# An fp32 conditioning layer with LoRA experts and a low-rank FFN: part of the transposes moved from TensorE to VectorE and the transfer queue

## The chip, the cores and the metric

The kernel runs on one core of a Trainium2 chip. The time is the device time of one execution in microseconds. The kernel before takes 154.18 us, the median of three runs (153.75 to 154.49). The profiled execution took 154.44 us.

The engines are named as in the profile: PE is TensorE, DVE is VectorE, ACT is ScalarE, POOL is GpSimd and SP is SyncE, which here only issues transfers.

## What is computed

There are 2048 tokens (32 x 64) of width 1024, in fp32. In short form:

```python
base   = x @ W.T                                   # (2048, 1024)
logits = x @ Wr.T + 5 * one_hot(language_id, 8)
gates  = softmax over the top 2 logits, 0 elsewhere
h      = einsum('btd,erd->bter', x, A)             # 8 experts, rank 16
cond   = base + 2 * einsum('bter,bte,eor->bto', h, gates, B)
out    = x + cond @ (U * S @ V.T).T                # rank 256
```

Only 256 numbers per token pass through the low rank. So the kernel forms the projection W.T V once (1024 x 256), and per token z = x (W.T V) + 2 (gates * h) (B V), and out = x + z (U S).T. B V, here bv, is 128 x 256.

## The kernel before, in words

**Precision.** PE multiplies in fp32r. Each fp32 operand is split into a rounded part (ACT, a copy, suffix hi) and the rest (DVE or POOL, a subtraction, suffix lo). Each product is three matmuls, `triple` (lines 342 to 345).

**Tiles.** 16 tiles of 128 tokens, worked on in 8 pairs (PAIRS). x^T of a tile comes from HBM into a ring of four (XTR), is split by ACT (split_x, line 609) and POOL (split_x, line 279). The plain x comes into x_all, a ring of six, and takes the result in place.

**Per tile**, `project(t)` (line 408) multiplies x^T as stationary operand by 264 columns: 128 for h, 8 for the logits, 128 for the first half of z. The result has tokens in the partitions, in bank pj[t % 2]. DVE turns the logits into gates in 11 small steps (gates_top, gates_apply, lines 772 to 804; one exponential on ACT, exp_top, line 661) and writes the gated h into gh.

**Per pair**, `half_t(p)` (line 425) forms the second half of z with the columns of z in the partitions, for both tiles at once. The last products need z this way round. The first half is in the other layout, so ACT copies it out of pj (copy_z, line 657) and PE transposes it into zt (line 434). In the same way gh is transposed (transpose_gh, line 442) into bank gt, split, and multiplied with bv onto zt (`mix`, line 450). mix(p) runs in the middle of project(2p + 2).

**The output product** uses Strassen's scheme in Winograd's form: 7 products of 128 x 128 x 512 (p1 to p7) where 8 would be plain. DVE forms four sums of z blocks (sums, line 827) and ACT and DVE split them (split_zb). `first_part(p)` is p1, p6, p7, p5, p2 and `second_part(p)` is p4, p3. p2 needs copy_u: ACT copies p1 out of bank_a before p2 is added there. DVE adds p6 and p7 to it (`up`, line 841), then adds the banks to x (xb1, xa0, xb0, xa1), and POOL adds the two upper sums (sides, line 306). The product lags two pairs behind the projections. The last pair is multiplied in the plain way (expand).

**Order.** Each engine has its own list, written out by hand, and waits on semaphores. PE's loop over pairs is lines 553 to 562: project(2p), first_part(p - 2), project(2p + 1), second_part(p - 2), zt_free(p), half_t(p), transpose_gh(p). ACT's is pair (line 665), DVE's pair_2 (line 876) and pair (line 893), POOL's lines 330 to 337. SP issues the loads and stores in the order of lines 242 to 250.

Of the kernel before, what the change touches and what calls it, by code (L numbers as in the profile page):

```python
# [16 lines left out]
def adaln_ffn(nc, xt, x, ids, VW, W, AW, B, U, S, out):  # L17
# [28 lines left out]
    with ExitStack() as ctx:  # L46
# [115 lines left out]
        x22_copied = sem("x22_copied")  # L162
# [178 lines left out]
        def _(pe):  # L341
# [66 lines left out]
            def project(t):  # L408
                q, r = t % 2, t % XTR
                pe.wait_ge(xt_lo, t + 1)  # L410
                if t >= 2:
                    pe.wait_ge(gh_done, t - 1)
                    pe.wait_ge(z_copied, t - 1)
                for k in range(DC):
# [6 lines left out]
                    if t >= 2 and t % 2 == 0 and k == MH:  # L421
                        mix(t // 2 - 1)
                last.then_inc(pj_done, 1)

            def half_t(p):
                r = (2 * p) % XTR
                dst = zt_v[:, 1, :, :]
                for k in range(DC):
                    last = triple(dst, proj_hi[:, k, TCOLS:COLS], proj_lo[:, k, TCOLS:COLS],
                                  xT_hi[:, r:r + 2, k, :], xT_lo[:, r:r + 2, k, :], k == 0, False, shared=True)  # L430
                    if k == MH + 1:
                        pe.wait_ge(z_copied, 2 * p + 2)
# [570 lines left out]
```

## Time and profile before

| | |
|---|---|
| median of three runs | 154.18 us |
| profiled execution | 154.44 us |
| its span, first to last instruction | 152.7 us |
| PE busy | 147.4 us, 97% |
| PE weight loads busy | 139.1 us, 91% |
| DVE busy | 107.2 us, 70% |
| POOL busy | 72.3 us, 47% |
| ACT busy | 63.5 us, 42% |
| moved by DMA | 32.72 MB, 214 GB/s on average |

A row of the time line gives the start in us from the span's start, how long it lasted, the engine, the line of the kernel, the operation, what it writes and reads with the shapes, and how many such instructions are merged in it. In brackets stands the idle time ahead and what ended it. The durations of matmuls overlap, so the step from start to start is what one costs. "q" behind an engine is its queue: there the duration is that of issuing a transfer. The table by stretch gives the stretch, its length, and per engine the busy us and the number of instructions (PE, PE's weight loads, DVE, ACT, POOL), then the clock granted to PE as a share of full speed, the DMA engines' busy share and GB/s.

### The profile page before, as it was taken

Reading aid. Unit: us, or ns where it says so; the run is one execution under the profiler, and the core shown is the slowest. Engines: PE = TensorE matmul, PEld = TensorE weight load, DVE = VectorE, ACT = ScalarE, POOL = GpSimd, SP = SyncE. Lnnn points to the kernel's source line nnn. Section 1 sums busy time; section 2 is a strip of 40 time slices with the busy share of each in tenths; the row PEclk is TensorE's granted clock in tenths of the full one; section 3 lists DMA queues with packets and bytes.
Section 4 is the critical chain, followed back from the end, with each engine's and each line's share of the span. In section 5 each row is a group of like instructions: output and inputs, shape, how many; then the busy total and the mean of one; then the engine's idle time right before and its main releaser. Section 6 shows DMA issues by size and latency. Waiting matters only on the chain.

```text
span 152.7 us, 2912 instructions
## 1 busy us (share of the span) xinstructions
PE 147.4 (97%) x1056; PEld 139.1 (91%) x1056; DVE 107.2 (70%) x297; ACT 63.5 (42%) x141; POOL 72.3 (47%) x57
## 2 busy tenths in 40 slices
PE   7799999999999999999999999999999999999991
PEld 5699999999999989998999899989999998998880
DVE  0488887759478999978765875587558736795851
ACT  4397876894546422446014612351334105013000
POOL 2000242993560659292966186636655640721700
PEclk9999999999999999999999999999999999999998
DMA  5999999999303030049719903980591068006184
GB/s 171 315 400 409 400 405 411 410 407 409 132 6 137 0 137 4 0 192 345 288 60 350 386 34 136 338 347 10 211 286 57 0 277 262 17 0 275 69 339 142
DMA packets 10670, 32.72 MB, mean 214 GB/s; under 512 B 1441, under 2 KB 1953, under 8 KB 10529
## 3 DMA queue, kind: packets, MB, share of 16 engines
q1 hardware_dynamic: 10368, 31.96, 55.8%
q10 hardware_dynamic: 288, 0.59, 1.2%
q8 instruction: 8, 0.13, 0.3%
q14 instruction: 6, 0.04, 0.1%
HBM read 24.16 MB, written 8.39 MB: 213 GB/s over the span
## 4 chain that ended last, share of the span: by engine, by line
PE 93%; DMA 3%; ACT 0%; DVE 0%; SPq 0%; issue 0%; DVEq 0%
PE fin L343 13%; PE fin L345 13%; PE fin L344 13%; PE pj L344 10%; PE pj L343 10%; PE pj L345 10%; PE zt L343 6%; PE zt L345 6%; PE zt L344 6%; DMA w_raw<-in_W 3%; PE gt L447 1%; PE zt L434 1%; PE fin L380 1%; PE gt L344 1%; PE gt L345 1%; PE fin L390 1%
## 5 line engine op out<-in xcount | busy, mean ns | idle before, releaser
L281 POOL TENSOR_TENSOR xT_lo<-xt_raw,xT_hi 128x1024 fp32r<-128x1024 f32 x15 | 36.5, 2443 | 25.2 <-DVE gh L801 7.9
L304 POOL TENSOR_TENSOR x_all<-x_all,vw_raw 128x512 f32<-128x512 f32 x21 | 26.6, 1297 | 25.8 <-DVE vw_raw L849 25.8
L343 PE MATMUL pj<-proj_hi,xT_hi 128*128 128x264 f32 x128 | 36.9, 288 | 0.0
L344 PE MATMUL pj<-proj_lo,xT_hi 128*128 128x264 f32 x128 | 36.3, 284 | 0.0
L345 PE MATMUL pj<-proj_hi,xT_lo 128*128 128x264 f32 x128 | 36.2, 283 | 0.0
L343 PE MATMUL fin<-v_hi,w_hi 128*128 128x256 f32 (+1 forms) x80 | 25.7, 321 | 0.0
L344 PE MATMUL fin<-v_lo,w_hi 128*128 128x256 f32 (+1 forms) x80 | 25.6, 320 | 0.0
L345 PE MATMUL fin<-v_hi,w_lo 128*128 128x256 f32 (+1 forms) x80 | 25.6, 320 | 0.0
L344 PEld LDWEIGHTS pj<-proj_lo,xT_hi 128*128 128x128 f32 x128 | 24.1, 189 | 0.2
L343 PEld LDWEIGHTS pj<-proj_hi,xT_hi 128*128 128x128 f32 x128 | 24.1, 188 | 0.2
L345 PEld LDWEIGHTS pj<-proj_hi,xT_lo 128*128 128x128 f32 x128 | 24.0, 188 | 0.0
L343 PE MATMUL zt<-xT_hi,proj_hi 128*128 128x256 f32 x64 | 18.6, 291 | 0.0
L855 DVE TENSOR_TENSOR x_all<-fin,x_all 128x512 f32<-128x512 f32 x28 | 17.9, 682 | 0.0
L344 PE MATMUL zt<-xT_lo,proj_hi 128*128 128x256 f32 x64 | 17.9, 280 | 0.0
L345 PE MATMUL zt<-xT_hi,proj_lo 128*128 128x256 f32 x64 | 17.9, 280 | 0.0
L613 ACT CAST xT_hi<-xt_raw 128x1024 fp32r<-128x1024 f32 x16 | 16.8, 1048 | 0.6 <-DMA xt_raw<-in_xt 0.5
L345 PEld LDWEIGHTS fin<-v_hi,w_lo 128*128 128x128 f32 x80 | 15.2, 191 | 1.2
L343 PEld LDWEIGHTS fin<-v_hi,w_hi 128*128 128x128 f32 x80 | 15.2, 190 | 0.9
L344 PEld LDWEIGHTS fin<-v_lo,w_hi 128*128 128x128 f32 x80 | 15.2, 190 | 0.8
L659 ACT COPY z_sb<-pj 128x128 f32<-128x128 f32 x16 | 4.3, 266 | 22.4 <-DVE logit L776 22.4
L344 PEld LDWEIGHTS zt<-xT_lo,proj_hi 128*128 128x128 f32 x64 | 12.0, 188 | 0.3
L343 PEld LDWEIGHTS zt<-xT_hi,proj_hi 128*128 128x128 f32 x64 | 12.0, 188 | 0.2
(100 smaller groups left out, 282.5 us busy)
## 6 DMA issues: line engine op xcount, KB each, us to landing
xt_raw<-in_xt SPq DMA_DIRECT2D x16, 512.0 KB, 7.6
x_all<-in_x SPq DMA_DIRECT2D x16, 512.0 KB, 6.5
out<-x_all SPq DMA_DIRECT2D x13, 512.0 KB, 3.2
vw_raw<-in_VW SPq DMA_DIRECT2D x6, 384.0 KB, 7.1
w_raw<-in_W SPq DMA_DIRECT2D x8, 256.0 KB, 6.6
out<-x_all SPq DMA_DIRECT2D x5, 256.0 KB, 2.0
w_raw<-in_U SPq DMA_DIRECT2D x1, 1024.0 KB, 8.8
aw_raw<-in_AW SPq DMA_DIRECT2D x1, 544.0 KB, 7.2
```

The lines of the kernel that those rows point to most:

```text
L281: nc.gpsimd.tensor_sub(xT_lo[:, t % XTR, :, :], xt_raw[:, t % XTR, :, :], xT_hi[:, t % XTR, :, :].bitcast(F32)).then_inc(xt_lo, 1)
L304: nc.gpsimd.tensor_add(x_all[:, t % XR, cols], x_all[:, t % XR, cols], ups[:, j, :]).then_inc(side_add, 1)
L343: nc.tensor.matmul(dst, l_hi, r_hi, start=first, stop=False, skip_group_check=shared)
L344: nc.tensor.matmul(dst, l_hi, r_lo, start=False, stop=False, skip_group_check=shared)
L345: return nc.tensor.matmul(dst, l_lo, r_hi, start=False, stop=last, skip_group_check=shared)
L380: nc.tensor.matmul(p_dst(h, m), w_hi[:, i % WRING, cols], v_hi[:, k, :], start=False, stop=False, skip_group_check=True)
L390: last = nc.tensor.matmul(p_dst(h, m), w_lo[:, i % WRING, cols], v_hi[:, k, :], start=False, stop=True, skip_group_check=True)
L434: nc.tensor.matmul(zt_v[:, 0, t, :], z_sb[:, t, :], ident[:, :], start=False, stop=False, is_transpose=True, skip_group_check=True)
L447: last = nc.tensor.transpose(gt[:, t * P:(t + 1) * P], gh[:, t, :], ident[:, :])
L613: nc.scalar.copy(xT_hi[:, t % XTR, :, :], xt_raw[:, t % XTR, :, :]).then_inc(xt_hi, 1)
L659: nc.scalar.copy(z_sb[:, t % 2, :], pj[t % 2][:, Z0:TCOLS]).then_inc(z_copied, 1)
L855: nc.vector.tensor_add(x_all[:, t % XR, cols], src[:, :], x_all[:, t % XR, cols]).then_inc(fin_read, 1)
```

## The change

- In pairs 1 to 6 neither z nor gh is transposed by PE. DVE transposes their 32 x 32 blocks in place of the whole (turn_z from PSUM, turn_gh from SBUF) into blk. SP moves the 12 blocks off the diagonal to their place in tr with 12 transfers of 32 x 4 x 128 bytes a pair, ACT copies the 4 on the diagonal.
- gh is split from tr (split_gh_moved), and mix(p - 1) runs in pair p behind first_part(p - 2). The first half of z is added to zt in PSUM by DVE (add_z0) behind it. z has two banks (zt and gt) now, so that two pairs can be under way.
- The z split of a pair follows a pair later, in two steps: the first takes three blocks (split_z_parts), the second four. The four sums read their operands from PSUM.
- half_t(p) runs directly behind the two projections. x^T is loaded and split a pair sooner (POOL's waits between the splits go).
- Pair 0 and pair 7 keep PE's transposes.

The core of the diff; SQ is 32, SQS 4 and MOVES 192:

```diff
+        zs = w_flat[:, 0:8 * P].rearrange("p (j n) -> p j n", n=P)
+        blk = w_flat[:, 8 * P:16 * P].rearrange("p (q m n) -> p q m n", q=2, m=4)
+        tr = w_flat[:, 16 * P:24 * P].rearrange("p (q m n) -> p q m n", q=2, m=4)
...
         bv_ps = gt[:, RANK:2 * RANK]
-        zt_v = zt[:, :].rearrange("p (m t n) -> p m t n", m=MC, t=2)
+        zt_bank = [zt, gt]
+        zt_v = [b[:, :].rearrange("p (m t n) -> p m t n", m=MC, t=2) for b in zt_bank]
...
+            def move_blocks(p):
+                sp.wait_ge(blk_done, 3 * p)
+                for i in range(SQS):
+                    for j in range(SQS):
+                        if i != j:
+                            sp.dma_start(tr[SQ * j:SQ * (j + 1), p % 2, :, SQ * i:SQ * (i + 1)],
+                                         blk[SQ * i:SQ * (i + 1), p % 2, :, SQ * j:SQ * (j + 1)]).then_inc(tr_load[p % 2], 16)
+
             for p in range(1, PAIRS):
-                if 2 * p + XTR < TILES:
-                    load_xt(2 * p + XTR)
-                    load_xt(2 * p + 1 + XTR)
+                if p == 1:
+                    load_xt(2 + XTR)
+                    load_xt(3 + XTR)
+                if 2 * p + 2 + XTR < TILES:
+                    load_xt(2 * p + 2 + XTR)
+                    load_xt(2 * p + 3 + XTR)
+                if p < PAIRS - 1:
+                    move_blocks(p)
                 if 2 * p >= XR:
                     load_x(2 * p)
                     load_x(2 * p + 1)
...
-            pool.wait_ge(tl_done, 2)
             split_x(5)
             pool.wait_ge(us_lo_done, MC)
+            split_x(6)
+            split_x(7)
             for p in range(2, PAIRS):
-                if p < PAIRS - 1:
-                    split_x(2 * p + 2)
+                if p < PAIRS - 2:
+                    split_x(2 * p + 4)
                 sides(p - 2)
-                if p < PAIRS - 1:
-                    pool.wait_ge(gh_done, 2 * p + 2)
-                    split_x(2 * p + 3)
+                if p < PAIRS - 2:
+                    split_x(2 * p + 5)
...
                     pe.wait_ge(gh_done, t - 1)
+                if 2 <= t < 4:
                     pe.wait_ge(z_copied, t - 1)
...
-                    if t >= 2 and t % 2 == 0 and k == MH:
-                        mix(t // 2 - 1)
+                    if t == 2 and k == MH:
+                        mix(0)
...
-                    if k == MH + 1:
-                        pe.wait_ge(z_copied, 2 * p + 2)
+                    if k == MH - 1 and p == PAIRS - 1:
+                        mix(p - 1)
+                    if k == MH + 1 and (p == 0 or p == PAIRS - 1):
+                        pe.wait_ge(z_copied, 2 if p == 0 else 4)
...
             def zt_free(p):
-                pe.wait_ge(za_lo, p)
-                pe.wait_ge(sums_done, 4 * p)
+                if p == 1:
+                    pe.wait_ge(bv_lo_done, 1)
+                if p >= 2:
+                    pe.wait_ge(za_lo, p - 1)
+                    pe.wait_ge(sums_done, 4 * (p - 1))
...
                 project(2 * p)
+                project(2 * p + 1)
+                zt_free(p)
+                half_t(p)
                 if p >= 2:
                     first_part(p - 2)
-                project(2 * p + 1)
+                if 3 <= p < PAIRS - 1:
+                    mix(p - 1)
+                if p == PAIRS - 1:
+                    transpose_gh(p)
                 if p >= 2:
                     second_part(p - 2)
-                zt_free(p)
-                half_t(p)
-                transpose_gh(p)
+                if p == 2:
+                    mix(1)
...
+            def split_z_parts(p):
+                act.wait_ge(z0_done, p)
+                zh_free(p)
+                nc.scalar.copy(zh[:, p % 2, 0:MC, :], zt_v[p % 2][:, :, 0, :])
+                nc.scalar.copy(zh[:, p % 2, MC, :], zt_v[p % 2][:, 1, 1, :])
+                nc.scalar.copy(zs[:, MC, :], zt_v[p % 2][:, 1, 1, :]).then_inc(za_hi, 1)
...
+            def split_gh_moved(p):
+                act.wait_ge(tr_load[p % 2], MOVES * ((p + 1) // 2))
+                act.wait_ge(tr_diag, SQS * p)
+                nc.scalar.copy(ghT_hi[:, :], tr[:, p % 2, 0:2, :]).then_inc(gt_hi, 1)
+
+            def move_diagonal(p):
+                act.wait_ge(blk_done, 3 * p)
+                for i in range(SQS):
+                    rows = slice(SQ * i, SQ * (i + 1))
+                    nc.scalar.copy(tr[rows, p % 2, :, rows], blk[rows, p % 2, :, rows]).then_inc(tr_diag, 1)
 
...
             def pair(p):
-                if p < PAIRS - 1:
-                    split_x(2 * p + 2)
-                split_za(p - 1)
-                copy_x22(p - 1)
+                exp_top(2 * p)
+                exp_top(2 * p + 1)
+                if p >= 3:
+                    split_gh_moved(p - 1)
+                if p < PAIRS - 2:
+                    split_x(2 * p + 4)
                 copy_u(p - 2)
+                if p == 2:
+                    split_gh_moved(1)
+                move_diagonal(p)
+                split_z_parts(p - 1)
+                if p < PAIRS - 2:
+                    split_x(2 * p + 5)
+                split_zb(p - 1)
+
+            def last_pair(p):
                 copy_z(2 * p)
                 exp_top(2 * p)
-                split_zb(p - 1)
-                if p < PAIRS - 1:
-                    split_x(2 * p + 3)
+                split_gh_moved(p - 1)
                 copy_z(2 * p + 1)
                 exp_top(2 * p + 1)
+                split_z_parts(p - 1)
+                copy_u(p - 2)
+                split_zb(p - 1)
                 split_gh(p)
...
             split_t(1)
-            copy_z(2)
+            split_x(5)
             exp_top(2)
             split_zb(0)
-            copy_z(3)
             exp_top(3)
-            split_x(5)
-            split_gh(1)
-            for p in range(2, PAIRS):
+            move_diagonal(1)
+            split_x(6)
+            split_x(7)
+            for p in range(2, PAIRS - 1):
                 pair(p)
+            last_pair(PAIRS - 1)
...
+            def turn_z(t):
+                nc.vector.transpose(blk[:, (t // 2) % 2, 2 + t % 2, :], pj[t % 2][:, Z0:TCOLS]).then_inc(blk_done, 1)
+
+            def turn_gh(p):
+                dve.wait_ge(gh_done, 2 * p + 2)
+                nc.vector.transpose(blk[:, p % 2, 0:2, :], gh[:, :, :]).then_inc(blk_done, 1)
...
+            def split_gh_moved(p):
+                dve.wait_ge(gt_hi, p + 1)
+                nc.vector.tensor_sub(ghT_lo[:, :].rearrange("p (t n) -> p t n", t=2), tr[:, p % 2, 0:2, :],
+                                     ghT_hi[:, :].bitcast(F32).rearrange("p (t n) -> p t n", t=2)).then_inc(gt_lo, 1)
...
+            def sums_first():
+                nc.vector.tensor_add(zs[:, 3, :], zt_v[0][:, 0, 1, :], zs[:, 2, :]).then_inc(sums_done, 1)
+                dve.wait_ge(sums_done, 1)
+                nc.vector.tensor_sub(zs[:, 4, :], zs[:, 3, :], zt_v[0][:, 0, 0, :]).then_inc(sums_done, 1)
+                dve.wait_ge(sums_done, 2)
+                nc.vector.tensor_sub(zs[:, 5, :], zs[:, 2, :], zs[:, 4, :]).then_inc(sums_done, 1)
+                nc.vector.tensor_sub(zs[:, 6, :], zt_v[0][:, 1, 0, :], zs[:, 4, :]).then_inc(sums_done, 1)
...
+            def add_z0(p):
+                dve.wait_ge(zt_done, p + 1)
+                dve.wait_ge(tr_load[p % 2], MOVES * ((p + 1) // 2))
+                dve.wait_ge(tr_diag, SQS * p)
+                nc.vector.tensor_add(zt_v[p % 2][:, 0, :, :], zt_v[p % 2][:, 0, :, :], tr[:, p % 2, 2:4, :]).then_inc(z0_done, 1)
 
             def sums(p):
                 n = 4 * p
-                nc.vector.tensor_add(zs[:, 1, :], zt_v[:, 0, 1, :], zs[:, 0, :]).then_inc(sums_done, 1)
+                z = zt_v[p % 2]
+                dve.wait_ge(za_hi, p + 1)
+                nc.vector.tensor_add(zs[:, 3, :], z[:, 0, 1, :], zs[:, MC, :]).then_inc(sums_done, 1)
...
-                nc.vector.tensor_sub(zs[:, 3, :], zs[:, 0, :], zs[:, 2, :]).then_inc(sums_done, 1)
-                nc.vector.tensor_sub(zs[:, 4, :], zt_v[:, 1, 0, :], zs[:, 2, :]).then_inc(sums_done, 1)
+                nc.vector.tensor_sub(zs[:, 5, :], z[:, 1, 1, :], zs[:, 4, :]).then_inc(sums_done, 1)
+                nc.vector.tensor_sub(zs[:, 6, :], z[:, 1, 0, :], zs[:, 4, :]).then_inc(sums_done, 1)
+
+            def split_z_parts(p):
+                nc.vector.tensor_sub(zl[:, p % 2, 0:MC, :], zt_v[p % 2][:, :, 0, :],
+                                     zh[:, p % 2, 0:MC, :].bitcast(F32))
+                nc.vector.tensor_sub(zl[:, p % 2, MC, :], zt_v[p % 2][:, 1, 1, :],
+                                     zh[:, p % 2, MC, :].bitcast(F32)).then_inc(za_lo, 1)
...
+            def gates(t):
+                gates_top(t)
+                if 2 <= t < TILES - 2:
+                    turn_z(t)
+                gates_apply(t)
+
             def pair_2():
                 split_zb(0)
                 split_us(1)
-                split_za(1)
+                gates(4)
+                gates(5)
+                turn_gh(2)
                 up(0, 1)
                 up(0, 2)
                 xb1(0)
-                sums(1)
-                gates_top(4)
-                gates_apply(4)
-                gates_top(5)
-                gates_apply(5)
+                split_gh_moved(1)
                 xa0(0)
                 xb0(0)
+                add_z0(1)
                 xa1(0)
-                split_gh(2)
+                sums(1)
+                split_z_parts(1)
 
             def pair(p):
+                gates(2 * p)
                 split_zb(p - 2)
-                split_za(p - 1)
-                sums(p - 1)
-                gates_top(2 * p)
-                gates_apply(2 * p)
+                gates(2 * p + 1)
+                turn_gh(p)
+                split_gh_moved(p - 1)
                 up(p - 2, 1)
                 up(p - 2, 2)
                 xb1(p - 2)
                 xa0(p - 2)
-                gates_top(2 * p + 1)
-                gates_apply(2 * p + 1)
+                add_z0(p - 1)
+                xb0(p - 2)
+                sums(p - 1)
+                split_z_parts(p - 1)
+                xa1(p - 2)
+
+            def last_pair(p):
+                gates(2 * p)
+                split_zb(p - 2)
+                split_gh_moved(p - 1)
+                gates(2 * p + 1)
+                add_z0(p - 1)
+                sums(p - 1)
+                up(p - 2, 1)
+                up(p - 2, 2)
+                xb1(p - 2)
+                xa0(p - 2)
+                split_z_parts(p - 1)
+                split_zb(p - 1)
+                split_gh(p)
                 xb0(p - 2)
                 xa1(p - 2)
-                if p == PAIRS - 1:
-                    split_zb(p - 1)
-                split_gh(p)
...
-            sums(0)
-            gates_top(2)
-            gates_apply(2)
-            gates_top(3)
-            gates_apply(3)
+            sums_first()
+            gates(2)
+            gates(3)
+            turn_gh(1)
             split_t(1)
-            split_gh(1)
             pair_2()
-            for p in range(3, PAIRS):
+            for p in range(3, PAIRS - 1):
                 pair(p)
+            last_pair(PAIRS - 1)
```

## Rows read from the trace of the kernel before

**Rows 1.** Section 1 of the page: busy time, share of the span, instructions.
```profile
PE 147.4 (97%) x1056; PEld 139.1 (91%) x1056; DVE 107.2 (70%) x297; ACT 63.5 (42%) x141; POOL 72.3 (47%) x57
```

**Rows 2.** Table by stretch, pair 2's stretch and a later pair's.
```profile
50.00:64.50 14.50, 14.50 (x105) 13.65 (x104) 13.36 (x33) 5.23 (x13) 8.79 (x6) 1.00 0.10 37
79.10:93.68 14.58, 14.58 (x105) 13.73 (x105) 9.71 (x33) 5.04 (x13) 8.64 (x6) 1.00 0.59 216
```

**Rows 3.** Time line of PE, the transposes of z and gh of pair 1.
```profile
49.29 0.28 PE L345 MATMUL zt<-xT_hi,proj_lo 128*128 128x256 f32 x1
49.40 0.38 PE L434 MATMUL zt<-ident,z_sb 128*128 128x128 f32 x2
...
49.74 0.28 PE L344 MATMUL zt<-xT_lo,proj_hi 128*128 128x256 f32 x1
...
50.34 0.38 PE L447 MATMUL gt<-ident,gh 128*128 128x128 f32 x2
```

**Rows 4.** Time line of PE, first and last product of two runs of 15.
```profile
43.28 0.28 PE L343 MATMUL pj<-proj_hi,xT_hi 128*128 128x264 f32 x1
...
44.97 0.28 PE L345 MATMUL pj<-proj_hi,xT_lo 128*128 128x264 f32 x1
...
54.17 0.40 PE L343 MATMUL fin<-us_hi,w_hi 128*128 128x512 f32 x1
...
57.35 0.39 PE L345 MATMUL fin<-us_hi,w_lo 128*128 128x512 f32 x1
```

**Rows 5.** Time line of DVE between 46 and 61 us.
```profile
46.08 0.15 DVE L776 SCALAR_TENSOR_TENSOR logit<-target,pj 128x8 f32<-128x8 f32 x1
...
46.59 0.23 DVE L781 TENSOR_SCALAR dtop<-top 128x2 f32<-128x2 f32 x1
...
46.99 0.17 DVE L784 TENSOR_TENSOR chosen<-iota_e,top_i 128x16 f32<-128x16 f32 x1
...
47.92 0.15 DVE L776 SCALAR_TENSOR_TENSOR logit<-target,pj 128x8 f32<-128x8 f32 x1
...
54.06 1.21 DVE L759 TENSOR_TENSOR us_lo<-vw_raw,us_hi 128x1024 fp32r<-128x1024 f32 x1
...
55.81 1.49 DVE L849 TENSOR_TENSOR vw_raw<-fin,vw_raw 128x512 f32<-128x512 f32 x2 [0.20 <-PE fin L345]
...
57.81 0.28 DVE L829 TENSOR_TENSOR zs<-zt,zs 128x128 f32<-128x128 f32 x1
...
59.78 0.55 DVE L781 TENSOR_SCALAR dtop<-top 128x2 f32<-128x2 f32 x1
...
60.50 1.10 DVE L784 TENSOR_TENSOR chosen<-iota_e,top_i 128x16 f32<-128x16 f32 x1
```

**Rows 6.** Time line of POOL between 43 and 62 us.
```profile
43.40 2.41 POOL L281 TENSOR_TENSOR xT_lo<-xt_raw,xT_hi 128x1024 fp32r<-128x1024 f32 x1 [1.16 <-DVE v_lo L812]
51.06 2.40 POOL L281 TENSOR_TENSOR xT_lo<-xt_raw,xT_hi 128x1024 fp32r<-128x1024 f32 x1 [5.25 <-DVE v_lo L812]
55.35 2.41 POOL L281 TENSOR_TENSOR xT_lo<-xt_raw,xT_hi 128x1024 fp32r<-128x1024 f32 x1 [1.90 <-DVE us_lo L759]
57.71 3.85 POOL L304 TENSOR_TENSOR x_all<-x_all,vw_raw 128x512 f32<-128x512 f32 x3
```

**Rows 7.** Time line of ACT between 43 and 56 us.
```profile
43.90 1.06 ACT L623 CAST v_hi<-vw_raw 128x1024 fp32r<-128x1024 f32 x1
...
48.69 0.20 ACT L663 ACTIVATE etop<-dtop 128x2 f32<-128x2 f32 x1 [0.32 <-DVE dtop L781]
48.89 1.04 ACT L613 CAST xT_hi<-xt_raw 128x1024 fp32r<-128x1024 f32 x1
...
55.06 0.59 ACT L651 COPY vw_raw<-fin 128x512 f32<-128x512 f32 x1 [0.62 <-PE fin L345]
```

**Rows 8.** Time line of SP's queue, the x^T loads of one pair.
```profile
66.93 2.02 SPq L202 DMA_DIRECT2D xt_raw<-in_xt  x2
```

**Rows 9.** Table by stretch, behind PE's last product, which ends at 149.3.
```profile
151.00:151.50 0.50, 0.00 (x0) 0.00 (x0) 0.00 (x0) 0.00 (x0) 0.00 (x0) 0.71 0.28 88
```

More of the change, by code:

```diff
@@ L157, in adaln_ffn @@
         gt_done = sem("gt_done")
+        blk_done = sem("blk_done")
+        tr_load = [sem("tr_load0"), sem("tr_load1")]
+        tr_diag = sem("tr_diag")
         gt_hi = sem("gt_hi")
@@ L161, in adaln_ffn @@
         zt_done = sem("zt_done")
-        x22_copied = sem("x22_copied")
+        zb_copied = sem("zb_copied")
+        z0_done = sem("z0_done")
         sums_done = sem("sums_done")
@@ L181, in adaln_ffn @@
         LAG = 4
+        SQ = 32
+        SQS = P // SQ
+        MOVES = 16 * SQS * (SQS - 1)
         PRODS = 7
@@ L426, in half_t @@
                 r = (2 * p) % XTR
-                dst = zt_v[:, 1, :, :]
+                dst = zt_v[p % 2][:, 1, :, :]
                 for k in range(DC):
@@ L438, in zt_free @@
             def zt_free(p):
-                pe.wait_ge(za_lo, p)
-                pe.wait_ge(sums_done, 4 * p)
+                if p == 1:
[3 more added lines that the diff above has]
+                    pe.wait_ge(sums_done, 4 * (p - 1))
             def transpose_gh(p):
+                dst = gt if p == 0 else pj[0]
                 pe.wait_ge(gh_done, 2 * p + 2)
-                if p >= 1:
-                    pe.wait_ge(gt_lo, p)
                 for t in range(2):
-                    last = nc.tensor.transpose(gt[:, t * P:(t + 1) * P], gh[:, t, :], ident[:, :])
+                    last = nc.tensor.transpose(dst[:, t * P:(t + 1) * P], gh[:, t, :], ident[:, :])
                 last.then_inc(gt_done, 1)
@@ L455, in mix @@
                     cols = slice(m * P, (m + 1) * P)
-                    last = triple(zt[:, 2 * m * P:2 * (m + 1) * P], bv_hi[:, cols], bv_lo[:, cols],
+                    last = triple(zt_bank[p % 2][:, 2 * m * P:2 * (m + 1) * P], bv_hi[:, cols], bv_lo[:, cols],
                                   ghT_hi[:, :], ghT_lo[:, :], False, True, shared=True)
@@ L631, in split_za @@
                 zh_free(p)
[L632 removed]
+                nc.scalar.copy(zh[:, p % 2, 0:MC, :], zt_v[p % 2][:, :, 0, :]).then_inc(za_hi, 1)
+            def split_z_parts(p):
[4 more added lines that the diff above has]
+                nc.scalar.copy(zs[:, MC, :], zt_v[p % 2][:, 1, 1, :]).then_inc(za_hi, 1)
             def split_zb_plain(p):
                 act.wait_ge(za_lo, p + 1)
[L636 to L641 removed]
+                nc.scalar.copy(zh[:, p % 2, MC:2 * MC, :], zt_v[p % 2][:, :, 1, :]).then_inc(zb_hi, 1)
             def split_zb(p):
                 act.wait_ge(sums_done, 4 * p + 4)
[L645 removed]
+                if p == 0:
+                    nc.scalar.copy(zh[:, 0, 2:7, :], zs[:, 2:7, :]).then_inc(zb_hi, 1)
+                else:
+                    nc.scalar.copy(zh[:, p % 2, 3:7, :], zs[:, 3:7, :]).then_inc(zb_hi, 1)
+            def split_gh_moved(p):
[7 more added lines that the diff above has]
+                    nc.scalar.copy(tr[rows, p % 2, :, rows], blk[rows, p % 2, :, rows]).then_inc(tr_diag, 1)
             def copy_u(p):
@@ L653, in split_gh @@
             def split_gh(p):
-                act.wait_ge(gt_done, p + 1)
-                nc.scalar.copy(ghT_hi[:, :], gt_both).then_inc(gt_hi, 1)
+                act.wait_ge(gt_done, 1 if p == 0 else 2)
+                nc.scalar.copy(ghT_hi[:, :], (gt if p == 0 else pj[0])[:, 0:2 * P]).then_inc(gt_hi, 1)
             def copy_z(t):
@@ L721, in _ @@
             split_za(0)
-            copy_x22(0)
+            nc.scalar.copy(zs[:, 2, :], zt_v[0][:, 1, 1, :]).then_inc(zb_copied, 1)
             split_t(1)
-            copy_z(2)
+            split_x(5)
             exp_top(2)
             split_zb(0)
-            copy_z(3)
             exp_top(3)
-            split_x(5)
-            split_gh(1)
-            for p in range(2, PAIRS):
+            move_diagonal(1)
+            split_x(6)
+            split_x(7)
+            for p in range(2, PAIRS - 1):
                 pair(p)
+            last_pair(PAIRS - 1)
             copy_u(PAIRS - 2)
@@ L837, in split_zb @@
                 dve.wait_ge(zb_hi, p + 1)
-                nc.vector.tensor_sub(zl[:, p % 2, 2:7, :], zs[:, :, :],
-                                     zh[:, p % 2, 2:7, :].bitcast(F32)).then_inc(zb_lo, 1)
+                first = 2 if p == 0 else 3
+                nc.vector.tensor_sub(zl[:, p % 2, first:7, :], zs[:, first:7, :],
+                                     zh[:, p % 2, first:7, :].bitcast(F32)).then_inc(zb_lo, 1)
             def up(p, j):
```

24 lines of the change are left out of this document (8 added, 16 removed).

## The prediction

> **What bounds the kernel now.** I read the page's busy times first: TensorE (PE) is busy for 147.4 of 152.7 us [rows 1]. The table by stretch then shows that this is no average over gaps: in a later pair (79.1 to 93.7) PE is busy 14.58 of 14.58 us, and in the stretch from 50 to 64.5 us 14.50 of 14.50, while VectorE (DVE) has 13.36 us of work there against 9.71 in that later pair [rows 2]. The reader is to see two things. Only PE work that disappears can shorten a pair; and the stretch in which pairs 1 and 2 meet is the one where a second engine is nearly full.
>
> The steps of PE come from start to start of instructions. One 264-wide product takes 0.121 us (14 steps from 43.28 to 44.97) and one 512-wide product 0.227 (14 steps from 54.17 to 57.35) [rows 4]. The 256-wide ones I put at 0.118. A pair is 48 x 0.121 + 30 x 0.118 + 21 x 0.227 = 14.1 us, and the rest of its 14.58, some 0.46, is four PE transposes.
>
> **What the change removes.** The two z transposes stand between starts 49.29 and 49.74: 0.45 us less two plain steps of 0.12 is 0.21; the pair sum above gives 0.23 [rows 3, 4]. The two gh transposes (first at 50.34) have the same shape. Both go in pairs 1 to 6: 12 x (0.21 to 0.24) = 2.5 to 2.9 us, taken as **2.7**. All of it is on the path, since PE has no gap there. Pairs 0 and 7 keep theirs. The two copies of z on ScalarE (ACT) that go cost nothing now: ACT waits.
>
> **What it adds on DVE, and the steady pairs 3 to 5.** Times here count from the first product of the pair. PE: two projections to 5.8, half_t to 8.6, five products to 12.0, the LoRA product (mix) to 12.7, two products to 14.1. New on DVE are turn_z (twice), turn_gh, add_z0, and one more part of the split. A DVE transpose has no row. The nearest are the 128x128 add from PSUM, 0.28 us, for turn_z, and between that and the 128x1024 subtraction, 1.21, for turn_gh [rows 5]; I take 0.3 and 0.4, of which 0.2 and 0.35 count from start to start. Bounds: 0.15 (a 128x8 operation) to 0.6 for each turn_z. Together with add_z0 that is about 1.5 us more in a pair of which DVE fills 9.7 of 14.6 us [rows 2]. It is hidden, if the order fits:
> Gates take 1.84 us (46.08 to 47.92) [rows 5], 2.05 with the turn. Gates of tile 2p start at 3.1. GpSimd (POOL) still splits the x of the pair before until about 4.6, which delays this gates' dtop (why, below). They end at about 5.9, the z split at 6.65, the second gates at 8.7, turn_gh at 9.1, the split of the moved gh at 9.5. POOL's next x split starts when half_t has freed x^T and ACT has split it, at 8.8 + 1.05 + 0.1 = 9.9 [rows 7]. So the gh split is through with 0.4 us to spare. ACT copies u at 9.9 to 10.4, the two sums from PSUM take 1.5 [rows 5] and are done at 12.0, before p4 at 12.7. add_z0, sums and z split follow and end at about 2.8 in the next pair. Nothing stalls PE; cost **0**. If the spare 0.4 us is gone, see rival 3.
>
> **Pair 2, the step that decides.** The new order puts POOL's splits of tiles 5, 6 and 7 earlier and back to back, and lets them fall on DVE's gates. The rows show what that does. With POOL idle dtop takes 0.23 us (46.59) and chosen 0.17 (46.99). While POOL runs three additions in a row (57.71, 3.85 for three, so they end at 58.99, 60.28, 61.56), dtop at 59.78 takes 0.55 and ends at 60.33, just behind the second; chosen at 60.50 takes 1.10 and ends at 61.60, just behind the third [rows 5, 6]. A DVE operation of these kinds waits for the end of the running POOL operation, and the next POOL operation gets in ahead of the one after. An x split holds POOL for 2.41 us [rows 6], so it can cost the gates twice that.
>
> The list, from the rows:
> - ACT's split_x(5) follows its split at 43.90 and is done at 45.9; POOL splits tile 5 at 46.0 to 48.4. Before, that split stood at 51.06, behind DVE's last v_lo [rows 6, 7]. Gates of tile 2 start at 46.08; dtop now ends at 48.4 and the gates at 49.85 instead of 47.92.
> - DVE then has gates(3) to 51.9, turn_gh to 52.3, split_t(1) 1.2, z split 0.8 (640 elements, between the rows), split_us(1) 1.2: end at 55.4. Before it was 54.06 + 1.21 = 55.27 [rows 5].
> - At 55.4 the last wait of POOL is met, and it splits tiles 6 and 7: 55.5 to 57.9, 57.95 to 60.35. (Before, one split stood at 55.35 and DVE had PSUM work beside it.) DVE comes with gates(4): dtop, due at 55.9, ends at 57.95; chosen waits to 60.35; the gates end at 61.5 instead of 57.4. gates(5): 61.5 to 63.55.
> - On ACT copy_u(0) now stands behind exp_top(5) and split_x(8). ACT is free 0.97 us after the gates begin (48.89 against 47.92) [rows 5, 7]: 62.5; split_x(8) to 63.5, copy_u(0) to 64.1.
> - PE: gh transposes at 50.34 [rows 3] less the 0.22 saved put project(4) at 50.1; two projections and half_t end at 58.7; p1, p6, p7, p5 end at 61.4. p2 needs copy_u(0) and starts at 64.15: **2.7 us** idle. The sums from PSUM end at 64.9 and 65.6; p4 was due at 64.8: **0.8** more. p3 is just met. mix(1) needs DVE's gh split, which comes at 66.2, when POOL (x split to 66.05) has started its first side addition, 1.28 us: gh ready at 67.85, **0.85** idle, or nothing if DVE gets in first.
> Together 3.5 to 4.35 us, taken as **3.9**. PE is full in the pairs after, so nothing is given back. Without any POOL block copy_u(0) would be ready at 60.5 and the stall would be zero: the price hangs on the block alone.
>
> **SP's queue.** Each pair gets 12 transfers of 16 KB, between the x^T loads and the x loads, behind a wait for turn_gh (9.1). x^T loads now run a pair ahead; their waits (POOL's splits of two tiles back) are met before. The stores of x behind the moves need xa1 at 16.8 anyway. An issue behind others takes 1.0 us (2.02 for two) [rows 8]; the lower bound is a third of that, since the moves carry little. At 0.45 the moves are issued by 14.5 and needed at 21.8 (ACT's gh split of the next pair), so cost 0. At 1.0 they are issued at 21.1, which is rival 4.
> The Trainium skill (DMA: Bandwidth & Descriptors, section Bandwidth) says that transfers under 64 KB are dominated by their descriptors, and its fit for one DMA (section Anatomy of one DMA) is about 2.0 us plus bytes over 436 GB/s. One after the other that makes 12 x 2.04 = 24.5 us a pair as an estimate, more than the pair has. The fit is for one transfer at a time, and no row here shows 16 KB transfers in a train; it is why rival 4 has a chance at all.
>
> **The end.** Pair 7 keeps its PE work. p1(6) needs a z split that ends at 14.4 of the pair, and is due at 14.55: 0. The next z split (two SBUF operands) is due at 14.35, and POOL's third side addition at 14.4, so p6(6) may wait up to 1.2 us: **0.6** taken, 0 and 1.2 kept.
>
> **Sum** against the profiled execution: span 152.7 - 2.7 + 3.9 + 0.6 = 154.5; around the span lie 154.44 - 152.7 = 1.74 us, so 156.24. The median shown, 154.18, is 0.26 under the profiled execution: **156.0**, 1.2% slower.
>
> **Rivals.**
> 1. No lock in pair 2 (the gates get in between, or POOL starts behind them), the transposes' gain stays: 152.7 - 2.7 + 1.74 - 0.26 = **151.5**. For it: VectorE's instructions are short, and half a microsecond in the order decides. Against: rows 59.78 and 60.50 show both waits, and POOL's start 0.08 after split_us (55.35 against 55.27) comes ahead of dtop, due 0.5 after. Chance 0.22.
> 2. Only the first of the two waits bites: gates(4) end at 59.25, copy_u(0) at 62.0; p2 0.6 late, p4 0.7. With 0.6 to 1.2 at the other places the gain is cancelled: **153.4 to 154.9**, no change. Chance 0.13.
> 3. The forecast and more: DVE's gh split in pairs 3 to 5 comes behind POOL's x split at 9.9 (turns of 0.45 us do it) and waits to 12.3; p4 then starts at 13.8 instead of 12.7, 1.1 us in each of three pairs, so **159.3**. Or PE's clock: it is at full speed to 151 us and at 0.71 in the half microsecond behind [rows 9], that is, it begins to fall to 1.2 from 2.4 GHz under two microseconds after PE's last product. An idle gap of 2.7 us could do the same; three microseconds at half speed would cost 1.5: **157.5**. Both are slower; 0.2 in all.
> 4. The moves are late. SP would need 12 x 1.0 + 5 = 17 us for a pair of 14.1; 3 us in five pairs: over **168**. Against it: the trains of full 512 KB loads are the slowest thing in the queue. Chance 0.05.
> The forecast itself, within 154.9 to 157: 0.4.
>
> **Numbers.** A measurement of this kernel can tell about 0.5% (0.77 us) from no change. Faster is rival 1 and the lucky edge of 2: 0.23. Same: 0.13. Slower: 0.64. The likeliest case alone ranges over 154.9 to 157.0; for 8 in 10 I need rival 1 at one end and the two of rival 3 nearly at the other: 151.3 to 158.6.
>
> **What would show it.** In the trace after: no transposes in pairs 1 to 6 and steady pairs of 14.1 us; dtop and chosen of tile 4 with 2 us each; the copy of u of pair 0 behind the exp of tile 5; a PE gap of 2 to 3 us in front of the second half of bank_a's sum near 61 to 64 us. Wrong would be: chosen of tile 4 with 0.17 us, PE without a gap there, a pair of 14.5 or more from 70 us on, or an ACT wait on tr_load.

## The result and the profile after

The changed kernel takes 155.01 us, the median of 20 runs (153.78 to 155.98); the kernel before takes 153.99 in 20 runs beside them (153.24 to 154.66). The ratio is 1.0069, 95% interval 1.0047 to 1.0092: slower, by more than chance, and by about half of the 1.2% forecast. Here and below a median is of all runs, and a ratio, with its 95% interval, leaves out runs more than 1.5% above the fastest of their kernel.

The profiled execution took 154.07 us with a span of 152.3, which is 0.4 us *less* than the span of before. That is no contradiction. The 20 runs fall into two groups by the mean clock that PE was granted: ten at 0.998 or more (153.78 to 155.83, median 154.27) and ten at 0.986 to 0.988 (155.01 to 155.98, median 155.67). The profile shows one of the first group.

Busy times on the page, and two stretches of 14 us (stretch, length, then PE, PE's weight loads, DVE, ACT, POOL, the granted clock, DMA share, GB/s). They answer to [rows 1] and [rows 2]. The second stretch lies in later pairs, where nothing stalls.

```profile
PE 145.6 (96%) x1032; PEld 136.0 (89%) x1032; DVE 118.4 (78%) x327; ACT 68.2 (45%) x159; POOL 72.1 (47%) x57
```

```profile
50.00:64.00 14.00, 11.64 (x82) 10.37 (x81) 13.16 (x34) 6.58 (x17) 6.84 (x3) 1.00 0.32 93
106.00:120.00 14.00, 14.00 (x100) 13.16 (x99) 11.02 (x39) 5.08 (x16) 7.58 (x5) 1.00 0.53 165
```

A late pair is as full of PE work as before, with 24 matmuls fewer in the whole kernel. From one p1 to the next it now takes 14.17 us (89.50 to 117.85 for two pairs), where before it took 14.58 (83.33 to 127.08 for three). The loss is all in the first stretch: PE works for 11.64 of 14 us. Its three gaps, in the time line of PE (the bracket gives the idle time and who ended it), are these:

```profile
62.46 0.47 PE L365 MATMUL fin<-us_hi,w_hi 128*128 128x512 f32 x1 [1.87 <-ACT vw_raw L699]
...
63.89 0.51 PE L365 MATMUL fin<-v_hi,w_hi 128*128 128x512 f32 x1 [0.49 <-DVE vw_raw L946]
...
65.87 0.39 PE L365 MATMUL gt<-ghT_hi,bv_hi 128*128 128x256 f32 x1 [0.32 <-DVE ghT_lo L881]
```

These are p2, p4 and mix(1). Measured from start to start, less the plain step, they cost 2.03, 0.66 and 0.48 us, 3.2 together. What is behind them stands in the lines of DVE, POOL and ACT, against [rows 5], [rows 6] and [rows 7]:

```profile
54.04 0.15 DVE L837 SCALAR_TENSOR_TENSOR logit<-target,pj 128x8 f32<-128x8 f32 x1
...
54.55 2.07 DVE L842 TENSOR_SCALAR dtop<-top 128x2 f32<-128x2 f32 x1
...
56.80 2.18 DVE L845 TENSOR_TENSOR chosen<-iota_e,top_i 128x16 f32<-128x16 f32 x1
...
59.83 0.15 DVE L837 SCALAR_TENSOR_TENSOR logit<-target,pj 128x8 f32<-128x8 f32 x1
...
62.34 1.49 DVE L946 TENSOR_TENSOR vw_raw<-fin,vw_raw 128x512 f32<-128x512 f32 x2
```

```profile
54.20 4.75 POOL L303 TENSOR_TENSOR xT_lo<-xt_raw,xT_hi 128x1024 fp32r<-128x1024 f32 x2 [6.78 <-DVE us_lo L820]
```

```profile
60.60 0.20 ACT L711 ACTIVATE etop<-dtop 128x2 f32<-128x2 f32 x1 [3.64 <-DVE dtop L842]
...
60.80 1.03 ACT L645 CAST xT_hi<-xt_raw 128x1024 fp32r<-128x1024 f32 x1
61.74 0.57 ACT L699 COPY vw_raw<-fin 128x512 f32<-128x512 f32 x1
```

The reader is to see that an operation on 128 x 2 numbers lasts 2.07 us and one on 128 x 16 lasts 2.18, that the first ends at 56.62 and the second at 58.98, and that POOL's two splits end at about 56.6 and 58.95. The gates of tile 4 take 5.8 us (54.04 to 59.83); those of tile 5, which meet no split, take 2.0. On ACT the exp, the x split and the copy of u follow one after the other behind the dtop of tile 5.

### The profile page after: what moved, and what is told of

It reads as the page before. It is cut to its first block, busy times and chain, and to the rows that moved or that the text cites. A ratio compares the mean times of both kernels' runs of the same rounds, so it can differ in the third digit from the quotient of the medians.

```text
span 152.3 us, 2976 instructions
## 1 busy us (share of the span) xinstructions
PE 145.6 (96%) x1032; PEld 136.0 (89%) x1032; DVE 118.4 (78%) x327; ACT 68.2 (45%) x159; POOL 72.1 (47%) x57
## 4 chain that ended last, share of the span: by engine, by line
PE 83%; DVE 12%; issue 1%; ACT 1%; DVEq 1%; POOL 0%; POOLq 0%
PE fin L365 12%; PE fin L367 12%; PE fin L366 12%; PE pj L366 8%; PE pj L365 8%; PE pj L367 8%; PE gt L365 3%; PE gt L367 3%; PE gt L366 3%; DVE dtop L842 3%; PE zt L367 3%; PE zt L365 2%; PE zt L366 2%; PE fin L567 2%; DVE chosen L845 2%
## 5 line engine op out<-in xcount | busy, mean ns | idle before, releaser
L303 POOL TENSOR_TENSOR xT_lo<-xt_raw,xT_hi 128x1024 fp32r<-128x1024 f32 x15 | 35.9, 2407 | 33.8 <-ACT xT_hi L645 20.3
L365 PE MATMUL pj<-proj_hi,xT_hi 128*128 128x264 f32 x128 | 36.4, 284 | 0.0
L326 POOL TENSOR_TENSOR x_all<-x_all,vw_raw 128x512 f32<-128x512 f32 x21 | 27.3, 1328 | 19.0 <-DVE vw_raw L946 19.0
L952 DVE TENSOR_TENSOR x_all<-fin,x_all 128x512 f32<-128x512 f32 x28 | 18.5, 683 | 1.2 <-POOL x_all L326 0.8
L711 ACT ACTIVATE etop<-dtop 128x2 f32<-128x2 f32 x16 | 3.3, 203 | 29.4 <-DVE dtop L842 29.4
L946 DVE TENSOR_TENSOR vw_raw<-fin,vw_raw 128x512 f32<-128x512 f32 x14 | 9.7, 690 | 6.6 <-ACT vw_raw L699 5.8
L365 PE MATMUL fin<-us_hi,w_hi 128*128 128x512 f32 (+1 forms) x31 | 11.9, 382 | 1.9 <-ACT vw_raw L699 1.9
L842 DVE TENSOR_SCALAR dtop<-top 128x2 f32<-128x2 f32 x16 | 10.6, 664 | 1.5
L367 PE MATMUL fin<-us_hi,w_lo 128*128 128x512 f32 (+1 forms) x31 | 11.7, 378 | 0.0
L366 PE MATMUL fin<-us_lo,w_hi 128*128 128x512 f32 (+1 forms) x31 | 11.7, 376 | 0.0
```

The costliest lines, as they stand in the source:

```text
L303: nc.gpsimd.tensor_sub(xT_lo[:, t % XTR, :, :], xt_raw[:, t % XTR, :, :], xT_hi[:, t % XTR, :, :].bitcast(F32)).then_inc(xt_lo, 1)
L326: nc.gpsimd.tensor_add(x_all[:, t % XR, cols], x_all[:, t % XR, cols], ups[:, j, :]).then_inc(side_add, 1)
L365: nc.tensor.matmul(dst, l_hi, r_hi, start=first, stop=False, skip_group_check=shared)
L366: nc.tensor.matmul(dst, l_hi, r_lo, start=False, stop=False, skip_group_check=shared)
L367: return nc.tensor.matmul(dst, l_lo, r_hi, start=False, stop=last, skip_group_check=shared)
L711: nc.scalar.activation(etop[:, :], dtop[:, :], ACT.Exp, accum_out=esum[:, :]).then_inc(exp_done, 1)
```

## The experiments

e1, e2, e3 and e5 are the changed kernel with one thing different, e4 is e1 and e7 is e6 with one thing more, and e6 changes several things at once. The kernel before ran beside them on the same chip: 153.57 us beside e1 to e4 (33 runs), 153.66 beside e5 to e7 (11 runs, on another chip). The changed kernel itself did not run beside them, so it is compared with them by the ratios to before and by the traces, and not by the medians.

**e1: POOL behind the gates.**

```diff
             pool.wait_ge(us_lo_done, MC)
+            pool.wait_ge(gh_done, 6)
             split_x(6)
             split_x(7)
```

> The changed kernel, but GpSimd splits the x of tiles 6 and 7 only after the gates of tile 5 (one wait more). Theory A (the shared port: GpSimd's two splits hold the gates of tile 4, and everything behind them waits): dtop and chosen of tile 4 fall from 2.07 and 2.18 us to about 0.23 and 0.17, the gap of 2.0 us in front of p2 of pair 0 goes; a smaller one of up to 1 us may come at mix(1), where DVE's gh split meets the split of tile 7. Span about 2 to 3 us under the changed kernel's 152.3, median 152 to 153. Theory B (the list of ACT: copy_u(0) stands behind the exp of tile 5 and the x split, whatever the gates do): the gap stays above 1.5 us. Theory C (DVE has simply too much work in this pair): the gap stays, since no DVE work goes.

Measured: 153.00 us, ratio to before 0.9967 (0.9943 to 0.9991), span 151.0. The gates of tile 4 in its DVE line:

```profile
54.41 0.23 DVE L843 TENSOR_SCALAR dtop<-top 128x2 f32<-128x2 f32 x1
...
54.82 0.17 DVE L846 TENSOR_TENSOR chosen<-iota_e,top_i 128x16 f32<-128x16 f32 x1
...
61.42 1.63 DVE L882 TENSOR_TENSOR ghT_lo<-w_raw,ghT_hi 128x256 fp32r<-128x256 f32 x1
```

0.23 and 0.17, and the gap before p2 is gone. No DVE work was taken away and ACT's list was left as it was, so B (ACT's list) and C (too much work) fall as causes. But of the 3.2 us only half came off: POOL now splits tiles 6, 7 and 8 in one go (57.99, 7.32 us) and the block moves to the gh split, 1.63 us for 0.4 of work. PE loses 0.65 at mix(1), 0.43 at half_t(3) and 0.51 at p2 of pair 1, 1.6 together. So the span is 1.3 us under the changed kernel's, where theory A had said 2 to 3.

**e2: ACT copies u at once.**

```diff
                 exp_top(2 * p)
+                if p == 2:
+                    copy_u(0)
                 exp_top(2 * p + 1)
...
-                copy_u(p - 2)
+                if p >= 3:
+                    copy_u(p - 2)
```

> The changed kernel, but in pair 2 ACT copies p1 out of the bank before the exp of tile 5 and the x split. Theory A: p2 is no longer late, but the two sums from PSUM stand behind the gates of tile 5 on DVE and are still ready only at about 62.3 and 63.8, so p4 starts at the same time as now (63.9) and the time stays within 0.3 us of the changed kernel. Theory B: the gap of 2.0 us goes and the kernel is 2 us faster.

Measured: 153.52 us, ratio 0.9999 (0.9973 to 1.0025). Four of its 12 runs have a lowered clock; e7 comes back to them. In the profile the copy of u is done at 59.3, and PE has one gap in place of three:

```profile
63.89 0.50 PE L365 MATMUL fin<-v_hi,w_hi 128*128 128x512 f32 x1 [2.50 <-DVE vw_raw L949]
```

p4 starts at 63.89, to the hundredth when it did in the changed kernel. So ACT's list names the releaser of the first gap but doesn't set the end of the chain; DVE's gates do. Only mix(1) came out better, by 0.5 us: DVE's gh split started at 64.352, 0.01 us ahead of POOL's first side addition, and took 0.41 us in place of 1.47. Nothing in the edit puts it there.

**e3: one split on the gates instead of two.**

```diff
             split_x(6)
+            pool.wait_ge(gh_done, 6)
             split_x(7)
+            pool.wait_ge(gt_lo, 2)
```

> The changed kernel, but only the split of tile 6 falls on the gates of tile 4; the one of tile 7 waits for the gates of tile 5, the one of tile 8 for DVE's gh split of pair 1. Theory A: dtop of tile 4 keeps about 2.07 us, chosen falls to 0.17; copy_u(0) is ready about 2 us earlier, just when p2 is due; p4 up to 0.7 us late, mix(1) 0 to 0.8. Span about 2 us under the changed kernel. Theory B and C: no more than 0.5 us.

Measured: 153.10 us, ratio 0.9967 (0.9947 to 0.9986), span 151.0.

```profile
54.55 2.06 DVE L844 TENSOR_SCALAR dtop<-top 128x2 f32<-128x2 f32 x1
...
56.79 0.18 DVE L847 TENSOR_TENSOR chosen<-iota_e,top_i 128x16 f32<-128x16 f32 x1
```

dtop is held as before and chosen is free: each POOL split costs the gates one wait, and the second one is the price of the 2 us gap. p4 was 0.67 late, as forecast for this case. Holding tile 8's split back made the side additions late, and DVE stood idle for 3.16 us before xb0; p2 of pair 1 was 0.51 late. So the span fell by 1.3 us here too, where about 2 was expected, and theories B and C allowed 0.5.

**e4: the removed transposes put back.** e1 with four transposes of a tile of zeros in each of pairs 1 to 6.

```diff
+                    if k == MH + 1 and 1 <= p < PAIRS - 1:
+                        for t in (0, 1, 0, 1):
+                            nc.tensor.matmul(zt_v[p % 2][:, 0, t, :], zeros[:, :].bitcast(F32), ident[:, :], start=False,
+                                             stop=False, is_transpose=True, skip_group_check=True)
```

> As e1, with four PE transposes of a tile of zeros put back into half_t of each of pairs 1 to 6 (they add zero to z). It prices what the change removes. Theory A and the sum of the prediction: 24 x 0.11 = 2.5 to 2.9 us over e1, pairs of 14.58 us again. Rival: part of the removed PE time only becomes waiting for DVE or GpSimd, and less than 1.5 us comes back.

Measured: 154.48 us, ratio 1.0056 (1.0037 to 1.0075), 1.5 us over e1. That is neither number. The pairs tell why: from p1 to p1 the late ones take 14.63 us against e1's 14.17, so four transposes cost 0.46 where PE is full. Around e1's gaps they cost nothing: from p1 of pair 0 to p1 of pair 1 e4 takes 15.20 us against e1's 15.51, since the gap of 0.65 at mix(1) is gone, and the next such stretch takes 15.16 in both, since half of the gap at p2 of pair 1 and the small waits around it went. The gain of the change is real in each full pair, and worth less next to a gap.

**e5: every move twice.**

```diff
-        MOVES = 16 * SQS * (SQS - 1)
+        MOVES = 2 * 16 * SQS * (SQS - 1)
...
+                            sp.dma_start(tr2[SQ * j:SQ * (j + 1), p % 2, :, SQ * i:SQ * (i + 1)],
+                                         blk[SQ * i:SQ * (i + 1), p % 2, :, SQ * j:SQ * (j + 1)]).then_inc(tr_load[p % 2], 16)
```

> The changed kernel with each of the 12 transfers of a pair issued twice, the second time to a place that nobody reads. It measures how much room the queue of SP has. In the changed kernel 12 moves take 7.7 to 8.7 us of issue. Theory A (the moves are hidden, SP has some 3 us of a pair free, none is paid for now): 24 moves take about 16 us, a pair can't be under 16 + 3.4 = 19 us once SP is the bound, and the kernel is 10 to 25 us slower; the wait is ACT's and DVE's for the moved blocks. Rival D (the transfer engines work the second ones off beside the first): under 2 us slower.

Measured: 193.02 us, ratio 1.253 (1.247 to 1.259). The longest waits of its trace (in total, times, longest):

```profile
ACT ghT_hi L690 <- DMA w_raw<-w_raw: 45.3, 6, 11.7
POOL xT_lo L306 <- ACT xT_hi L648: 43.5, 6, 12.6
DVE ghT_lo L884 <- ACT ghT_hi L690: 38.7, 6, 10.7
```

Theory A was right about the mechanism and too low in size: by the ratios to before, e5 is some 38 us slower than the changed kernel, in place of 10 to 25. One issue takes 0.64 us, so 24 take 15.5, and with loads and stores SP needs about 19.5 us a pair. Beyond that the wait sits in ACT's list ahead of the x split and the copy of u, so PE stops for 3.8 us at mix(1) in pair 2, for 3.2 to 6.6 us in each of pairs 3 to 6 and for 9.6 in pair 7, and the mean granted clock is 0.92. The changed kernel has no such wait: its moves are hidden, with less room than it looks.

**e6: POOL's work set between the gates.**

```diff
             split_x(6)
+            pool.wait_ge(gh_done, 6)
             split_x(7)
-            for p in range(2, PAIRS):
+            pool.wait_ge(gt_lo, 2)
+            sides(0)
+            split_x(8)
+            pool.wait_ge(gh_done, 7)
+            split_x(9)
+            for p in range(3, PAIRS):
...
                 exp_top(2 * p + 1)
+                if p == 2:
+                    copy_u(0)
...
-                copy_u(p - 2)
+                if p >= 3:
+                    copy_u(p - 2)
...
                 gates(5)
-                turn_gh(2)
                 up(0, 1)
                 up(0, 2)
                 xb1(0)
+                turn_gh(2)
```

> The changed kernel with GpSimd's work in pair 2 set by hand between DVE's gates: tile 6 as now, tile 7 behind the gates of tile 5, then pair 0's side additions behind the gh split, tile 8, and tile 9 behind the gates of tile 6; ACT copies p1 of pair 0 ahead of the x split, and turn_gh(2) stands behind the three sums. Theory A: the gaps that e1 and e3 kept (0.67 at p4 of pair 0, 0.2 at half_t(3), 0.5 at p2 of pair 1) go down to 0.5 us together, the span to about 150, the median 1.2 to 1.6 us under the kernel before. Rival: another wait takes their place and it stays at e3's 153.1.

Measured: 151.70 us, ratio **0.9886** (0.9868 to 0.9905), span 149.9. It beats the kernel before by 2.0 us, somewhat more than the 1.2 to 1.6 expected, and by its ratio the changed kernel as well (1.0069). Two gaps of 0.25 us are left, at p4 of pair 0 and p2 of pair 1. In POOL's line the split of tile 6 stands where it was, the one of tile 7 behind the gates of tile 5, and the side additions behind the gh split:

```profile
54.48 2.39 POOL L303 TENSOR_TENSOR xT_lo<-xt_raw,xT_hi 128x1024 fp32r<-128x1024 f32 x1 [6.78 <-DVE us_lo L829]
60.20 2.40 POOL L303 TENSOR_TENSOR xT_lo<-xt_raw,xT_hi 128x1024 fp32r<-128x1024 f32 x1 [3.32 <-DVE gh L878]
62.96 3.79 POOL L326 TENSOR_TENSOR x_all<-x_all,vw_raw 128x512 f32<-128x512 f32 x3 [0.36 <-DVE ghT_lo L890]
```

The first split still holds dtop of tile 4, and the DVE transpose of gh now falls into the second one:

```profile
54.83 2.07 DVE L851 TENSOR_SCALAR dtop<-top 128x2 f32<-128x2 f32 x1
...
62.03 0.43 DVE L864 STREAM_TRANSPOSE w_raw<-gh 128x256 f32<-128x256 f32 x1
```

So the waits need not all go: dtop of tile 4 is held for 2 us and PE stalls for no more than 0.25. Which of the edits of e6 gives how much was not taken apart.

**e7: one gap, to see the clock.** e6 with one wait of PE.

```diff
                 zt_free(p)
+                if p == 4:
+                    pe.wait_ge(gh_done, 10)
                 half_t(p)
```

> As e6, with one wait more: PE starts half_t of pair 4 only when the gates of tile 9 are done, so that a gap of about 2.3 us stands once among full pairs. Theory K (a gap of this size lowers PE's clock in part of the executions, which is the second cluster of the changed kernel's times): the mean granted clock is 0.985 to 0.99 in a third to a half of the runs, and these are 1.3 to 2 us over the others. Rival: the lower clock in the changed kernel came from something else; all runs at 0.997 or more and the time 2.3 us over e6 in each.

Measured: 157.23 us, ratio 1.024 (1.0216 to 1.0264). The gap came out at 3.5 us, not 2.3, and all six runs have a lowered clock: three at 0.989 (156.82 to 156.93), three at 0.975 (157.54 to 157.64). The profile is one of the first three. Its stretches around the gap (the clock is the third number from the end):

```profile
85.00:86.00 1.00, 0.00 (x0) 0.00 (x0) 0.91 (x4) 0.00 (x0) 0.00 (x0) 1.00 0.77 123
...
87.00:88.00 1.00, 0.09 (x1) 0.12 (x2) 0.90 (x6) 0.11 (x1) 0.00 (x0) 1.00 1.15 234
88.00:89.00 1.00, 1.00 (x6) 1.00 (x7) 0.55 (x2) 0.00 (x0) 0.00 (x0) 0.62 0.91 221
89.00:90.00 1.00, 1.00 (x7) 1.00 (x6) 0.00 (x0) 0.00 (x0) 0.00 (x0) 0.50 0.98 393
90.00:91.00 1.00, 1.00 (x7) 1.00 (x7) 0.00 (x0) 0.00 (x0) 0.00 (x0) 0.50 1.04 418
91.00:92.00 1.00, 1.00 (x8) 1.00 (x8) 0.00 (x0) 0.00 (x0) 0.00 (x0) 0.67 1.03 414
92.00:93.00 1.00, 1.00 (x8) 0.91 (x7) 0.00 (x0) 0.40 (x1) 0.00 (x0) 1.00 0.99 406
```

PE stands still from 84.6 to 87.9, which costs it 3.5 us from start to start. It resumes at full speed, falls to 0.5 (1.2 of 2.4 GHz) at about 88.2 and is back at about 91.6. There a 256-wide product steps by 0.21 us instead of 0.118. The span is 5.2 us over e6's: 3.5 are the gap, and the other 1.7 are what 3.4 us at half speed cost. No trace was kept of the runs at 0.975.

The changed kernel stands between: with a gap of 2.0 us and one of 0.7 behind it, ten of its 20 runs have the low clock, and e2 with one gap of 2.7 has four of 12 (0.978 to 0.989, 155.08 to 156.65, where the other eight are at 153.22 to 153.70). None of the 29 runs of e1, e3 and e6, with no gap over 0.7 us in pairs 0 to 7, is under 0.999, and none of e4's ten under 0.996. So theory K's mechanism holds, that a gap of PE lowers its clock; its share of the runs, a third to a half, was too low for the gap of 3.5 us that came about.

No trace was kept of a run of the changed kernel with the low clock, but e5's trace has the same two gaps in pair 2, 1.9 us at p2 and 0.66 at p4, and its clock falls right behind them. Later in the same trace PE stands still for 3.2 us, resumes at 107.85, and keeps its full clock:

```profile
65.00:66.00 1.00, 1.00 (x4) 0.76 (x4) 0.26 (x1) 0.00 (x0) 1.00 (x2) 0.54 0.12 16
66.00:67.00 1.00, 1.00 (x4) 0.56 (x2) 0.00 (x0) 0.00 (x0) 1.00 (x2) 0.50 0.08 12
...
107.00:108.00 1.00, 0.15 (x1) 0.15 (x2) 0.17 (x1) 0.99 (x3) 0.61 (x1) 1.00 1.35 340
108.00:109.00 1.00, 1.00 (x6) 0.87 (x7) 0.87 (x2) 0.89 (x3) 1.00 (x1) 1.00 0.73 172
109.00:110.00 1.00, 1.00 (x8) 0.80 (x7) 1.00 (x3) 0.00 (x0) 1.00 (x2) 1.00 0.99 254
```

A gap of 3.4 us there (PE resumes at 148.63) passes in the same way, while one of 3.7 (88.86) does not. So a gap makes the fall possible, and its length alone does not decide it, not even within one execution. What does stays open; no run here varies it alone.

## Why the prediction was right, and where its sizes were off

- **The mechanism of pair 2: right, step by step.** dtop 2.07 and chosen 2.18 us (forecast 2 each), the copy of u behind the exp of tile 5 and the x split, p2, p4 and mix(1) late in this order. e1 and e3 show that POOL's splits cause it, and e2 that the end of the chain does not hang on ACT's order.
- **Its price: 3.2 us, forecast 3.5 to 4.35.** p2 was 2.03 late instead of 2.7: the gates' waits end with POOL's splits, and that was at 58.98 instead of 60.35, 1.4 us sooner than in my list, while PE was only 1.0 us sooner; and the rest of the gates took 0.85 us (58.98 to 59.83) in place of 1.15. mix(1) lost 0.48 instead of 0.85: the gh split did meet a side addition, as listed (64.34, 1.47 us for 0.4 of work).
- **The transposes: 2.5 us, forecast 2.7.** 14.58 less 14.17 is 0.41 a pair, times six. e4, with four transposes put back, gives 0.46 a pair; where the 0.05 more come from was not traced.
- **The end: 0, forecast 0.6.** PE has no gap over 0.1 us behind pair 1. DVE's z split ran at 137.78 in 0.68 us without waiting. It seems, though no run shows it, that POOL waited instead: its three additions took 4.26 us from 135.36 on, where three take about 3.8 elsewhere.
- **Steady pairs: right that nothing stalls, but with more room than I gave.** In pair 4's time line DVE's gh split runs at 103.67 for 0.38 us and POOL's x split starts at 105.06: 1.0 us of room in place of 0.4. The block transposes take 0.31 (z) and 0.45 us (gh), as assumed.
- **The moves: hidden, but dearer.** 12 issues take 7.7 to 8.7 us, 0.64 each and more, where I took 0.45. Half of the 72 moves land within 1.86 us of their issue, and the next one is issued meanwhile, so the estimate of 24.5 us, one after the other, did not come true. The fit behind it is one that the Trainium skill (DMA: Bandwidth & Descriptors, "Anatomy of one DMA") gives for transfers that GpSimd issues, and SP issues these. Nothing in the trace waits for a move. e5 shows what would have happened with twice as many.
- **The start: not in the sum.** The profiled execution of before waited 0.87 us at 6.92 for its first weights, and the one after did not. The change does not touch this part, and in the other traces, where it is the same too, PE comes to this product anywhere from 6.04 to 7.13 us, so I take it as a difference between two executions and not of the change. Span 152.7 - 2.5 + 3.2 - 0.9 = 152.5, against 152.3 measured.
- **The clock: named as a rival, left out of the sum, and most of the result.** Without it the changed kernel is at 154.27 against 153.99, hardly slower; with it at 155.67. The median of 20 is between the two. The forecast of 156.0, less 1.3 (stall and end too large), plus 0.2 (the transposes' gain too large), less 0.6 (the start: 0.87, of which 0.26 was already taken off), is 154.3, the first group's 154.27. The low clock of half the runs lifts the median by 0.74 to 155.01. That this sum closes is in part luck, since it corrects a median by waits read from one trace of each kernel. The forecast came 1.0 us too high, and nearer than its terms were: with the terms of its sum as measured the kernel would be as good as unchanged (154.27 against 153.99, 0.2%). Most of the slowdown came from the clock, which the prediction had only in rival 3, at 1.5 us; the two groups lie 1.4 apart. So the mechanism of pair 2 was foreseen, and the size of the slowdown was met partly by luck.

## What to carry to other kernels

A change that takes work off the bounding engine has to be read against the stretch where another engine is nearly full, not against the average pair: there, the order of the helpers is worth more than the work removed, and e6 turned +0.7% into -1.1% (each against the kernel before beside it) with three waits and three steps moved. When work on GpSimd moves to an earlier place, list which VectorE operations with two SBUF operands, or of dtop's kind, it will now meet. A gap of two microseconds on TensorE may cost more than its length, and only in some of the executions, so look at the clock of every run before explaining a median by one profile.

## What the runs showed of the hardware

- A VectorE subtraction of a column (128 x 2, tensor_scalar) and operations on two SBUF tensors wait for the end of the GpSimd operation that is running, up to 2.0 us for a few numbers (2.07 and 2.18 us in place of 0.23 and 0.17). Operations with one operand in PSUM do not: the two sums of 62.34 take 1.49 us beside a GpSimd split, as in [rows 5]. Nor does the VectorE transpose of 128 x 256 from SBUF: in e6 it starts at 62.03, inside a GpSimd split that runs from 60.20 to 62.60, and takes 0.43 us, as it does with GpSimd idle (0.45 at 103.31 in the trace after). The Trainium skill (SBUF — State Buffer, "Who interferes with whom") has the VectorE instruction with two SBUF inputs, or in a 2-port mode, blocked fully by GpSimd and the one with at most one SBUF input left alone; by that rule, the traces agree (2.07 and 2.18 against 1.49 us for two sums).
- TensorE's clock fell after it had resumed: in e7 it worked at full speed for about 0.3 us behind the gap and then for some 3.4 us at half. In e5 the clock fell 1.8 us after PE had resumed behind the gap of 1.9 us (63.29 to about 65.1), did not fall behind gaps of 3.2 and 3.4 us, and fell inside the one of 6.6 us, at about 126.5.
- A 16 KB transfer within SBUF of 128-byte pieces takes SP 0.60 to 0.64 us to issue, more than a 512 KB load that finds the queue empty (0.33 us), and 1.8 to 1.9 us to land when no load is in flight. In a train of 12 they don't queue up behind each other, and the kernel waits for none of them. Behind 512 KB transfers they do wait: in pair 4, with loads and stores issued from 84.4 to 87.9, the first move of the train at 89.61 landed 6.3 us after its issue and the last 1.9.
